# All the 128-row tails ahead of all the late blocks in the expert stage of a graph layer with a mixture of experts

## The reference, cut to what matters

```python
def reference(x, adj, nodemask, ...):
    # x: 32 graphs of 256 nodes of 128 numbers, float32: 8192 tokens
    x = x + gnn(layernorm(x), adj, nodemask, W, b, a1, a2, att_b)
    x = x + ffn(layernorm(x), gate_w, gate_b, w1, b1, w2, b2, gamma, beta)
    return x

def ffn(x, ...):                                   # 16 experts, 2 of them for each token
    topk_vals, topk_idx = top_k(x @ gate_w + gate_b, 2)
    topk_w = softmax(topk_vals)
    h = relu(x @ w1[e] + b1[e])                    # 128 -> 256
    expert_out = h @ w2[e] + b2[e]                 # 256 -> 128
    y = x + sum over the two chosen e of topk_w * expert_out
    return (y - mean(y)) / sqrt(var(y) + 1e-5) * gamma + beta
```

## Time and profile before

| | before |
|---|---|
| median of three runs | 436.62 us (436.07 to 436.82) |
| the profiled execution | 438.15 us, span in the trace 436.4 us |
| busy in the span: PE, DVE, ACT, POOL | 341.8, 294.6, 228.4, 309.7 us |
| sends to token_y on POOL | 143, busy 144.7 us |
| granted TensorE clock, mean of the span | 0.944 |

### The profile page before, as it was taken

How to read it: one execution, slowest core, us unless ns; L and a number is a source line. 1 busy time by engine, 2 the same in 40 slices (tenths; PEclk the granted TensorE clock), 3 DMA queues, 4 the chain that set the end, 5 groups by cost and what they waited for, 6 DMA issues and landing times.

```text
span 436.4 us, 9782 instructions
## 1 busy us (share of the span) xinstructions
PE 341.8 (78%) x2289; PEld 280.1 (64%) x2289; DVE 294.6 (67%) x1445; ACT 228.4 (52%) x704; POOL 309.7 (71%) x343
## 2 busy tenths in 40 slices
PE   3897888758887766366998667888788898889991
PEld 2676777647876655254897557777677777734440
DVE  4778699999999996437777565666646465610674
ACT  2786898868999763311443233333333434411772
POOL 6634777776777777777777777777777777770575
PEclk9998899998999995559999999999999999999998
DMA  8932365554546475889977577776777867416994
GB/s 243 298 108 77 132 197 183 159 169 147 172 170 182 157 247 143 333 214 233 243 216 208 152 198 190 231 232 192 235 209 214 237 208 234 112 31 255 389 372 147
DMA packets 61674, 88.02 MB, mean 202 GB/s; under 512 B 10213, under 2 KB 40859, under 8 KB 61490
## 3 DMA queue, kind: packets, MB, share of 16 engines
q1 hardware_dynamic: 30786, 43.45, 34.5%
q0 software_dynamic: 10720, 25.32, 16.9%
q10 hardware_dynamic: 20112, 18.63, 14.6%
HBM read 55.61 MB, written 32.73 MB: 202 GB/s over the span
## 4 chain that ended last, share of the span: by engine, by line
PE 31%; DVE 25%; issue 13%; DMA 11%; POOL 6%; ACT 3%; ACTq 2%; SPq 1%; DVEq 1%; POOLq 1%
PE psum L1429 7%; PE psum L1440 6%; DMA token_y<-yb,xb 6%; POOL token_y L545 6%; DMA xb<-sorted_x 4%; PE psum L1483 3%; PE psum L1482 3%; DVE i L955 2%; PE psum L1341 2%; ACT xn L635 2%; DVE xmid L869 2%; PE psum L1419 2%; PE psum L1331 2%; DVE st L811 1%; PE psum L1488 1%
## 5 line engine op out<-in xcount | busy, mean ns | idle before, releaser
L545 POOL DMA_INDIRECT token_y<-yb,xb x143 | 144.7, 1012 | 43.6 <-issue 36.0
L519 POOL DMA_INDIRECT sorted_x<-xrow,rows x128 | 123.1, 962 | 42.8 <-issue 39.3
L702 ACT ACTIVATE hid<-psum,b_sb 128x256 f32<-128x256 f32 (+1 forms) x188 | 69.1, 419 | 127.2 <-PE psum L1429 112.9
L1429 PE MATMUL psum<-xbT,w_sb 128*128 128x256 f32 (+1 forms) x376 | 82.9, 344 | 7.8 <-DVE xbT L1186 5.7
L1440 PE MATMUL psum<-w_sb,hid 128*128 x572 | 82.1, 281 | 2.4 <-ACT hid L702 2.3
L1440 PEld LDWEIGHTS psum<-w_sb,hid 128*128 128x128 f32 x572 | 75.7, 194 | 8.3 <-issue 5.5
L1195 DVE TENSOR_TENSOR yb<-psum,b_bc 128x256 f32<-128x256 f32 (+1 forms) x94 | 33.8, 359 | 62.4 <-PE psum L1440 51.4
L1429 PEld LDWEIGHTS psum<-xbT,w_sb 128*128 128x128 f32 x376 | 57.9, 193 | 16.9 <-DVE xbT L1186 13.4
L1419 PE MATMUL psum<-ident_aug,xb 128*128 128x128 f32 x143 | 33.3, 290 | 20.9 <-DMA xb<-sorted_x 17.9
L1200 DVE SCALAR_TENSOR_TENSOR yb<-yb,xb 128x128 f32<-128x128 f32 x143 | 46.2, 351 | 3.3
L1186 DVE COPY xbT<-psum 128x256 f32<-128x256 f32 (+1 forms) x94 | 33.2, 353 | 10.1 <-PE psum L1419 9.8
(11 more groups left out here) (194 smaller groups left out, 578.5 us busy)
## 6 DMA issues: line engine op xcount, KB each, us to landing
xb<-sorted_x SPq DMA_DIRECT2D x49, 258.0 KB, 3.5
w_sb<-w_dram ACTq DMA_DIRECT2D x94, 128.0 KB
adj_in<-adj_dram SPq DMA_DIRECT2D x32, 256.0 KB
got<-token_y SPq DMA_DIRECT2D x12, 512.0 KB, 9.1
xb<-sorted_x SPq DMA_DIRECT2D x45, 129.0 KB, 3.1
out_dram<-xrow ACTq DMA_DIRECT2D x16, 256.0 KB, 4.7
xmid<-x_dram SPq DMA_DIRECT2D x6, 512.0 KB, 8.0
token_y<-yb,xb POOLq DMA_INDIRECT x143
```

The costliest lines, as they stand in the source:

```text
L519: pool.indirect_dma_start(sorted_x, bass.IndirectOffsetOnAxis(ap=rows[:, slot, t, k:k + 1], axis=0), xrow[:, slot, k, t, :], None).then_in ...
L545: pool.indirect_dma_start(token_y, bass.IndirectOffsetOnAxis(ap=xb[:, q, t, TO:TO + 1].bitcast(I32), axis=0), yb[:, h, t, :], None, bounds ...
L702: last = act.activation(hid[:, u % RING, c, 0:n], psum[:, 2 + u % 2, c * BT:c * BT + n], ACT.Relu, bias=b1_sb[:, c, e])
L1429: last = mm(psum[:, 2 + u % 2, c * BT:c * BT + n], w1_sb[:, u % IN_RING, c * P:(c + 1) * P], xbT[:, u % RING, 0:n], start=True, stop=True)
```

## The change

ORDER, the order of units 16 to 93, is now the 45 tails in a row and then the 33 blocks. Nothing else differs. Line numbers above 60 are lower by one in the changed kernel.

```diff
-ORDER = tuple(b for _, b in sorted([((2 * i + 1) / FULL, i) for i in range(FULL)]
-                                   + [((2 * i + 1) / TAILS, FULL + i) for i in range(TAILS)]))
+ORDER = tuple(range(FULL, FULL + TAILS)) + tuple(range(FULL))
```

## The result

The changed kernel takes 445.27 us (median of 4 runs, 444.72 to 445.92), the kernel before on the same chip 436.72 (4 runs): ratio 1.020, 95% interval 1.018 to 1.022. Slower, as forecast and within the range, but by 8.6 us where 5.3 were forecast. The profiled execution took 445.92 us with a span of 444.2, against 438.15 and 436.4 before, so the two traces differ by 7.8 us.

A forecast was written before the change was run, and what follows sets the result against it. POOL's 143 sends were taken to bound the second stage. Eight tails at 12.3 us against POOL's 10.5 gave 6.1 + 0.6 less 1.5 = 5.2 us, +5.3 with the end: 441.9 us, range 437.0 to 448.0.

The forecast's parts named there:

- POOL, its cushion and the place of the loss: Second stage: results ready 11.1 us before sending at unit 16 cover units 16 to 26; POOL then waits until unit 60.
- The cap on the cushion: From unit 27 the xb ring's 10.35 us turn against nine sends' 11.8 us leaves results at most 1.5 us ahead.
- PE's own work: On each tail PE's transpose and two layers take 0.11, 0.45 and 0.45: 1.01 us, 8.1 for eight.
- The reads: Register reads per eight tails: PE's adds 1.5 us, ACT's 1.6 on top, DVE's is hidden while PE waits for ReLU.
- The rival of hidden reads: Register reads overlap or cost only 587 ns, POOL stays fed, time unchanged at 436.7 us; chance 0.12.
- The adds, 1.1 for eight: Adds of beta on DVE each hold PE up by 0.4 us, 8/3 of them in eight units: 1.1 us.
- The 33 blocks cannot give this back: Blocks after the tails let results get ahead again, but POOL cannot go faster than its sends, so nothing is regained.
- The price of 1.315 for a send: Second stage: POOL's 188.0 us over 143 sends, 1.315 us each, a tail 1.315 and a block 2.63.
- the rival *faster: Adds falling into POOL's gaps would no longer slow sends, ending the second stage up to 4.6 us earlier, 432.1; chance 0.04.
- ended the loss with unit 60: Row of tails: the last loss is units 54 to 60, without adds, 7 x 0.085 = 0.6 us.
- The end: Start of the third stage: loads follow the last landing as before, PE's fillers finish later, costing 0.1 to 0.2 us.
- The slower ring: xb ring in the tails: DMA share 0.82, landing and load up 40%, 4.4 us lost, 441.0; chance 0.18.

The follow-up runs named there:

- the adds in the blocks: Changed kernel with long reads kept, its sixteen adds of beta moved behind every second block: 445.58 us, ratio 1.0179.
- short reads: Changed kernel with the tails' table entries moved from 33 to 40, so batches of eight begin at a multiple of eight: 439.11 us, ratio 1.0051.
- short reads and adds last: Changed order with tails' entries at a multiple of eight and the sixteen adds of beta behind the last unit: 436.87 us, ratio 1.0018.
- the fillers in it: Changed kernel plus one filler matmul on PE ahead of the transposes of units 20 to 25: 446.06 us, ratio 1.0201.
- PE with ACT: Changed order with the tails' entries moved to 40, but PE and ACT start one entry off and stay long: 444.33 us, ratio 1.0185.
- PE with DVE: Changed order with the tails' entries moved to 40, but PE and DVE start one entry off and stay long: 446.09 us, ratio 1.0218.
- PE alone: Changed order with the tails' entries moved to 40, but only PE starts one entry off and stays long: 442.63 us, ratio 1.0158.
- even mix with short reads: Kernel before with adds of beta behind the last unit and entries arranged so batches begin at a multiple of eight: 434.71 us, ratio 0.9943.

## Why the prediction was right in sign and short in size

**POOL, its cushion and the place of the loss: right.** The sends came without gaps up to unit 29, then starved up to unit 60 and the first block, with lumps of about 1.5 us, and then never again. The cap on the cushion held: unit 16's result lay ready 10.5 us before its send, units 25 to 28 only 1.9 to 2.2, and from unit 30 on 0.8 to 1.3. When POOL waits, 0.85 us lie between result and send, so the cushion of units 25 to 28 is 1.1 to 1.3, against 1.5 at most.

**PE's own work, "1.01 us, or 8.1 for eight": too small.** This is the step that failed most. The prediction priced both layers at 0.45 from one pass in front of a read the earlier trace rows, and took the second from the first because that pass has no transpose right behind it. A plain pass takes 0.11 + 0.50 + 0.54 = 1.15 (262.40 to 263.55 with the adds in the blocks): 1.1 us more for eight, 0.14 on every tail of the starved stretch, 31 x 0.14 = 4.3 us. Why the pass in front of a read is shorter was not followed.

**The reads: right.** With the adds in the blocks PE's 1.5 measured 1.65, ACT's 1.6 measured 1.48, and DVE's is hidden, as counted, in the kernels with all three long. The rival of hidden reads fell because the reads ahead of tails stayed long; its own condition, 0.6 us for a read, was made true in the run with short reads, and its outcome then came within 2.6 us in the median (ratio 1.0051 where it said no change).

**The adds, 1.1 for eight: too large.** In the changed kernel two of the batches took 12.97 and 13.01 us on PE (from 261.87 to 274.84 and to 287.85), 0.65 above the 12.32 without adds.

**The clock: not foreseen.** The third batch took 14.08 (287.85 to 301.93). Between 294 and 300 the granted clock was 0.71, 0.50 and 0.94 in stretches of 2 us. The three average 13.35, which is the 1.67 of each tail that POOL shows. So eight tails took 9.2 for PE's work, 3.1 for the reads, 0.65 for the adds and some 0.35 for the clock, where the forecast had 8.1, 3.1, 1.1 and nothing.

**"The 33 blocks cannot give this back": partly wrong.** The price of 1.315 for a send held the sends that adds slow. Behind the last add, at unit 53, a send takes 0.98 + 0.30, and the blocks' sends gave back 1.4 us. The mechanism of the rival *faster* was real (2.6 us of busy time less) and too small against the wait. It is partly luck that the sum was only 3.3 us short: the adds priced too high and this gain, not counted, stand against PE's work priced too low.

**The step to the first block: not foreseen.** The forecast ended the loss with unit 60. Of the 1.3 us that units 54 to 60 lost, where it had 0.6, 1.06 are the wait of the first block's send at 315.45.

**The end: right up to the first pair.** SP's first load and the first weights of a pair, in the changed kernel:

```profile
402.25 2.97 SPq L445 DMA_DIRECT2D got<-token_y  x6
...
406.95 0.19 PEld L1481 LDWEIGHTS psum<-got,ident_aug 128*128 128x128 f32 x1 [0.24 <-issue]
```

POOL's last send ends at 400.80, so 1.45 us pass up to the load and 4.70 from there to the pair, where it was 1.31 and 4.66: 0.2 us more, as counted. The other 0.5 to 0.6 us of the 0.7 lie in the third stage itself, behind the first pair, and were not followed.

**The slower ring: refuted.** The loads of a tail's rows took 2.7 us from issue to landing in the median of the changed profile; the ring held PE up between 236 and 251 us, as it cut the cushion. In the starved stretch PE's long idle times ahead of transposes lie beside its reads (from 259.7, 272.6 and 285.7, about 2.0 us each), none at a load of rows:

```profile
261.87 0.30 PE L1418 MATMUL psum<-ident_aug,xb 128*128 128x128 f32 x1 [1.35 <-issue]
...
274.84 0.30 PE L1418 MATMUL psum<-ident_aug,xb 128*128 128x128 f32 x1 [1.52 <-DVE xbT L1185]
...
287.85 0.30 PE L1418 MATMUL psum<-ident_aug,xb 128*128 128x128 f32 x1 [1.56 <-issue]
```

With short reads the DMA share over the tails rises above the 0.82 that this rival priced, and POOL is fed all the same. The changed kernel, then the one with short reads:

```profile
260.00:312.00 52.00, 41.22 (x291) 36.04 (x290) 31.72 (x104) 20.36 (x64) 32.15 (x34) 0.97 0.73 208
...
260.00:312.00 52.00, 47.25 (x348) 41.93 (x347) 36.72 (x118) 23.59 (x72) 39.52 (x39) 1.00 0.85 246
```

**What stays open:** with short reads and adds last the order of the change is still 0.75% behind the mix (1.0018 against 0.9943, some 3 us by these ratios), and the profiles account for 1.6 us of gaps and 0.9 at the end, less 1.1 by an earlier start. The 2.6 us that short reads alone leave in the median do not show in the execution that was profiled.

## What to carry to other kernels

When units of one size are put in a row, price a whole batch by the distance between the same instruction of two neighbouring passes in the trace, not by adding durations; stalls that a cushion hid in a mix then add up one behind another. Before blaming the order, look for a stall that can be removed: here a table position that makes eight register entries begin at a multiple of eight was worth three quarters of the loss. And an instruction that is off the critical path can still slow the one on it: moving sixteen adds away from POOL's sends made the even mix itself 0.55% faster.

## What the runs showed of the hardware that was not expected

A register read of eight entries takes 588 to 599 ns on PE where they begin at a multiple of eight in the table, and about 2.0 us where they begin one entry behind it, the only other position that was run; two tails cost PE 2.30 us and a block of the same rows 1.97 (317.10 to 319.07 in the changed kernel).

In the profiled executions PE's granted clock fell to 0.50 (1.2 GHz) in the starved part of the row of tails in the kernels in which PE's read was long (the change, the fillers in it, PE with ACT, PE with DVE: once between 258 and 316 us; PE alone: twice; with the adds in the blocks: never), and in none of the four in which it was short. As it began to fall PE had been busy 0.57 of 2.00 us in one case and 0.96 of 2.00 in another, each with one or two pauses of 0.6 to 1.4 us. But the pauses of 1.52 and 1.56 us at 274.84 and 287.85 brought no fall, nor did the same reads in the mix. A long read is not needed for it: in the even mix with short reads the clock was 0.50 from 288 to 290 us, behind a wait for rows of 2.48 us. Why one does and another does not was not settled.
